# One transposing transfer per attention head in place of two, in an attention, MLP and top-k kernel on one core

## The chip, the cores and the metric

The kernel runs on one core of one Trainium2 chip. The metric is the device time of one execution in microseconds (us); a comparison takes the median of several runs.

## The reference

The input x has four sequences of 512 rows by 512 columns. The first stage adds a 0/1 mask to x: per sequence, the 5120 largest entries of softmax(x) times an outer product, without the diagonal. The second stage is a transformer block with modulated layer norms, sixteen heads of width 128, and an MLP of width 2048 with an exact gelu.

```python
adj = emb_s * emb_t * (softmax(x) / sqrt(n)); adj[diag] = -inf
x = x + one_hot(top_k(adj.flat, 5120))
x1 = ln(x) * (1 + scale1) + shift1
q, k, v = split(x1 @ qkv_w + qkv_b)                 # 16 heads of 128
attn = softmax(einsum('bthd,bshd->bhts', q, k) * DH ** -0.5)
x = x + gate1 * (einsum('bhts,bshd->bthd', attn, v) @ out_w + out_b)
x = x + gate2 * (gelu(ln2(x) @ ffn_w1 + ffn_b1) @ ffn_w2 + ffn_b2)
```

The case's function returns its input plus the block's result once more, and the same weights serve all four sequences.

## The kernel before

Every 32-bit operand is held as a high and a low part, and each product is three matmuls (`mm3`, L1387 to L1389). The four sequences run one after the other (0 to 3); each has a head stage of sixteen heads, an output projection and an MLP. The top-k search of the next sequence is spread over the current one on VectorE and ScalarE. The four 128-row tiles of a head are called row tiles, two of them a pair (`PAIRS` is 2).

TensorE's order is written out by hand. In head h it does the scores of h, the query and key projection of h+1, a v tile or a part of the output projection, and then `attend` of head h-1, which multiplies the transposed probabilities `probT` by v. In head 14 and head 15 there is less to do between the scores and `attend`: head 15 has no projection of a next head, so that `attend` of head 14 follows its scores sooner than in the heads before it. `attend` of head 15 comes later, in the middle of the output projection.

The probabilities of a head reach `probT` in these steps:

- VectorE takes the row maxima (L1217), ScalarE the exponentials (L884), VectorE the reciprocals (L1228).
- ScalarE writes the high float16 half of each row tile into `halves16` (L891). Before the first it waits until the transfers of the head before have landed, since `halves16` is a single buffer for heads 0 to 12 and another for 13 to 15. VectorE writes the low half (L1232) and counts `p16_lo` after each row tile.
- SyncE's queue issues the transposing transfers into `turned16` (L537, function `turn`). Before them it waits for `widened` of the head before and for `p16_lo`.
- GpSimd copies `turned16` into `probT` as 32-bit values, one instruction for each pair (L741, function `widen`), after the pair's transfer has landed and `attend` of the head before is done (`pv_done`). `attend` waits for both.

SyncE's queue works in order. In sequences 1 to 3 the weight loads (`w<-split_weights`, L466) stand between the `turn` of one head and the next. In sequence 0 the weights are split on the chip: after each `turn` come loads of raw weights (`load_raw`, L449) and saves of split ones (L441), each released by a split on GpSimd (L661), which in turn follows a copy on ScalarE (L820). Heads 3, 7, 11 and 15 of sequence 0 have three splits, the others one; the last of the three stands behind `widen` in GpSimd's queue, and ScalarE's copy for it stands ahead of the next head's exponentials.

Of the kernel before, what the change touches and what calls it, by code (L numbers as in the profile page):

```python
# [52 lines left out]
NT = T // P  # L53
# [15 lines left out]
PAIRS = NT // 2  # L69
# [159 lines left out]
def block_kernel(nc, x, cond, weights, ada_w, cols, out):  # L229
    ctx = ExitStack()  # L230
    with ctx:
# [95 lines left out]
        def halves_of(h):  # L327

            return halves16[h >= TURNED_IN_V]

        def turned_of(h):

            return turned16[h >= TURNED_IN_V]
# [12 lines left out]
        def sem(name):  # L346
            return ctx.enter_context(nc.semaphore(name))
# [12 lines left out]
        q_lo, k_lo, v_lo, o_lo = sem("q_lo"), sem("k_lo"), sem("v_lo"), sem("o_lo")  # L360
        scores, nbias_ready, exp_done = sem("scores"), sem("nbias_ready"), sem("exp_done")
        rinv_ready, p16_hi, p16_lo = sem("rinv_ready"), sem("p16_hi"), sem("p16_lo")
        turned_in, widened = [sem("turned_in0"), sem("turned_in1")], sem("widened")
        y_done, y_gated, y_back = sem("y_done"), sem("y_gated"), sem("y_back")
        var_ready, std_ready, z_ready = sem("var_ready"), sem("std_ready"), sem("z_ready")
        zt_done, xt_full, xt_hi, xt_lo = sem("zt_done"), sem("xt_full"), sem("xt_hi"), sem("xt_lo")
# [29 lines left out]
        def wait_apart(eng, signal, value):  # L396


            eng.wait_ge(signal, value)
            eng.sem_inc(waits_met, 1)  # L400
# [32 lines left out]
        def _(sp):  # L433
# [96 lines left out]
            def turn(b, h):  # L530

                k = b * H + h
                for pair in range(PAIRS):
                    if k:
                        wait_apart(sp, widened, (k - 1) * PAIRS + pair + 1)
                    wait_apart(sp, p16_lo, k * NT + 2 * (pair + 1))
                    sp.dma_start_transpose(  # L537
                        turned_of(h)[:, 2 * pair:2 * pair + 2, :, :].rearrange("p i n t -> p (i n) t"),
                        halves_of(h)[:, 2 * pair:2 * pair + 2, :, :].rearrange("p i a s -> p (i a s)"))\
                        .then_inc(turned_in[pair], 16)  # L540

            def first_sequence():
                load_raw(2, AHEAD + 2)
# [11 lines left out]
                for h in range(H):  # L555
                    turn(0, h)
                    if h == H - 1:
                        load_x_again(1)
                    load_raw(at + 2, at + 2 + len(first_splits(h)))
                    at += len(first_splits(h))  # L560
# [17 lines left out]
            def sequence(b, last=False):  # L578
# [7 lines left out]
                for h in range(2, H):  # L586
# [4 lines left out]
                    if h == 14:  # L591
                        load_unit(b, 0)
                    load_qk(b, h)
                turn(b, H - 3)
                load_unit_half(b, 1, 0)
                turn(b, H - 2)
# [35 lines left out]
        def _(pool):  # L632
# [101 lines left out]
            def widen(b, h):  # L734

                k = b * H + h
                for pair in range(PAIRS):
                    wait_apart(pool, turned_in[pair], 16 * (k + 1))
                    pool.wait_ge(pv_done, b * H + h)
                    rows = slice(2 * pair * P, 2 * (pair + 1) * P)  # L740
                    nc.gpsimd.tensor_copy(  # L741
                        probT[:, :, :, rows].rearrange("p a j (i t) -> p i (a j) t", i=2),
                        turned_of(h)[:, 2 * pair:2 * pair + 2, :, :]).then_inc(widened, 1)
# [19 lines left out]
        def _(act_e):  # L763
            def topk_exp(t):

                for i in range(NT):
                    act_e.wait_ge(xmax_ready, t * NT + (i + 1))
                    nc.scalar.activation(adj[:, i, :], adj[:, i, :], ACT.Exp, bias=nxmax[:, i:i + 1],
                                         accum_out=nxsum[:, i:i + 1]).then_inc(xexp_done, 1)

            def topk_count(t, step):

                at = count_split(t)
                src = keys16[:, at:, 1] if step < LEVEL else low[:, at:]
                if t == 1 and step == 0:
                    act_e.wait_ge(rows_saved, 16)
                act_e.wait_ge(cand_ready, t * (STEPS + 1) + (step + 1))
                with nc.allow_low_precision(reason=EXACT):
                    nc.scalar.activation(passed_s[:, :2 * NCOUNT - at], src, ACT.Sign, bias=cand[:, :], scale=-1.0,  # L779
                                         accum_out=cnt_s[:, :]).then_inc(counted_s, 1)  # L780
# [51 lines left out]
            def split_qk(b, h):  # L832

                if h >= 2:
                    split_hi(b, qk_half(h), k_done, b * H + (h - 1))
                else:
                    split_hi(b, qk_half(h), y2_tile, b * OUT_TILES)

            def split_unit(b, u, *halves_of_it):

                for half in halves_of_it or (0, 1):
                    n = unit_half(u, half)
                    if u == 0:
                        split_hi(b, n, v_done, b * H + H)
                    elif u == 1:
                        split_hi(b, n, k_done, b * H + H)
                    elif u in (2, 3) and half == 0:
                        split_hi(b, n, pv_done, b * H + (H - 2 if u == 2 else H))
                    elif u < 6:
                        split_hi(b, n, y_done, b * Y_PIECES + (u - 1 if u < 5 else Y_PIECES))  # L850
                    elif u < 10:
                        split_hi(b, n, f_done, b * KC + 4 * (u - 5))
                    else:
                        split_hi(b, n, y2_half, b * OUT_HALVES + (2 * (u - 10) + half + 1))

            def v_part(b, idx):
                act_e.wait_ge(v_done, b * H + (idx + 1))
                if b and idx == 0:

                    act_e.wait_ge(y2_added, b * OUT_TILES)  # L860
                if idx == QUAD:

                    act_e.wait_ge(out_stored, b * 16 + STORE_CREDIT)
                if idx in (2 * QUAD, 3 * QUAD):

                    act_e.wait_ge(pv_done, b * H + idx - QUAD)
                bk = bank[4 + idx] if idx < 4 else bank[7]
                nc.scalar.mul(v[:, (idx // 4) % 2, 0, idx % 4, :], bk[:, :], V_DOWN).then_inc(v_hi, 1)

            def qk_part(b, h):  # L870
                act_e.wait_ge(q_done, b * H + (h + 1))
                nc.scalar.activation(qk[:, 0, 0, :], bank[4 if h else 1][:, :], ACT.Identity,
                                     bias=col("bq", h))\
                    .then_inc(q_hi, 1)
                act_e.wait_ge(k_done, b * H + (h + 1))
                nc.scalar.activation(qk[:, 1, 0, :], bank[5 if h else 2][:, :], ACT.Identity,  # L876
                                     bias=col("bk", h))\
                    .then_inc(k_hi, 1)

            def head(b, h, last):  # L880
                k = b * H + h
                for i in range(NT):
                    act_e.wait_ge(nbias_ready, b * (H * NT) + (h * NT + i + 1))
                    nc.scalar.activation(prob[:, i, :], bank[i][:, :], ACT.Exp, bias=nbias[:, i:i + 1],  # L884
                                         scale=SCALE, accum_out=rowsum[:, i:i + 1]).then_inc(exp_done, 1)
                if k:
                    for pair in range(PAIRS):
                        act_e.wait_ge(turned_in[pair], 16 * k)
                for i in range(NT):
                    act_e.wait_ge(rinv_ready, k * PAIRS + i // 2 + 1)  # L890
                    nc.scalar.mul(halves_of(h)[:, i, 0, :], prob[:, i, :], rinv[:, i:i + 1]).then_inc(p16_hi, 1)  # L891
                if h + 1 < H:
                    qk_part(b, h + 1)
                if h + 2 < H:
                    split_qk(b, h + 2)
                else:
                    split_unit(b, 1, h - (H - 2))
                if FIRST_TOTAL <= h + 1 and not last:
                    topk_count(b + 1, h + 1 - FIRST_TOTAL)
                if h + QUAD < H:  # L900
                    v_part(b, h + QUAD)
                if h == 0 and not last:
                    topk_exp(b + 1)
                refill(b, h, 0)
                if h:
                    o_part(b, h - 1)
                refill(b, h, 1)

            def o_part(b, h):
                act_e.wait_ge(pv_done, b * H + (h + 1))  # L910
                nc.scalar.activation(act[:, 0, h, :], bank[6][:, :], ACT.Identity, bias=col("bv", h))\  # L911
                    .then_inc(o_hi, 1)

            def refill(b, h, half):

                if h in (3, 7):
                    split_v(b, h // QUAD + 2, half)
                elif h == 11:
                    split_unit(b, 0, half)

            def sequence(b, last=False):
# [8 lines left out]
                for h in range(H):  # L930
                    head(b, h, last)
# [839 lines left out]
```

## Time and profile before

| what | value |
|---|---|
| median of 3 runs | 1572.07 us (1571.55 to 1572.12) |
| profiled execution | 1573.86 us, its span 1572.0 us |
| TensorE (PE) busy | 1508.5 us, 96% |
| VectorE (DVE), ScalarE (ACT), GpSimd (POOL) busy | 1110.1, 886.3, 409.9 us |
| granted TensorE clock, mean | 0.996 |
| queue q1 (all transfers from SyncE) | 325.90 MB, 69.3% of 16 engines' span |

SPq in a row is SyncE's queue issuing a transfer; the second number of a timeline row is how long the instructions took together, and a bracket at its end holds the idle time before it and what ended it. A row ending in x2 is two instructions back to back. Lines (L537) are those of the kernel before.

### The profile page before, as it was taken

What the parts mean: (1) busy time and instruction counts of PE and PEld (TensorE: products, weight loads), DVE (VectorE), ACT (ScalarE), POOL (GpSimd) and SP (SyncE); (2) the same over time, 40 slices, a digit from 0 to 9 for tenths busy, and PEclk for the clock granted to TensorE, in tenths of its full rate; (3) what the DMA queues carried; (4) which work ended last, traced back from release to release, by engine and by line L of the source; (5) the groups of instructions that cost most, each with busy time, mean ns of one, the idle gap of its engine ahead of it and who ended that gap; (6) DMA issues with size and microseconds to landing.
All of it is one profiled execution on the core that took longest, in us unless ns stands there. A gap on an engine that the chain in (4) does not pass through costs nothing.

```text
span 1572.0 us, 21300 instructions
## 1 busy us (share of the span) xinstructions
PE 1508.5 (96%) x7253; PEld 1250.4 (80%) x7253; DVE 1110.1 (71%) x2328; ACT 886.3 (56%) x1631; POOL 409.9 (26%) x243
## 2 busy tenths in 40 slices
PE   1999889999999999999999999999999999999998
PEld 1877778778778888887878888887978888888987
DVE  7878978876786887775775887775777666664431
ACT  4557577774754666663672766664572556554240
POOL 6713635454120322221000232221000122222000
PEclk9999999999999999999999999999999999999999
DMA  7867869998666788685455777677454787776463
GB/s 289 314 242 195 237 171 261 247 219 299 216 231 238 170 214 215 165 206 176 175 219 205 199 207 208 163 214 208 168 201 170 220 201 160 209 210 156 176 237 123
DMA packets 334507, 327.58 MB, mean 208 GB/s; under 512 B 270752, under 2 KB 275008, under 8 KB 331328
## 3 DMA queue, kind: packets, MB, share of 16 engines
q1 hardware_dynamic: 334112, 325.90, 69.3%
q8 instruction: 58, 0.95, 0.2%
q14 instruction: 49, 0.40, 0.1%
q10 hardware_dynamic: 288, 0.33, 0.1%
HBM read 204.54 MB, written 54.54 MB: 165 GB/s over the span
## 4 chain that ended last, share of the span: by engine, by line
PE 87%; DVE 7%; DMA 2%; DVEq 1%; ACT 1%; issue 1%; SPq 1%; POOL 0%; ACTq 0%; POOLq 0%
PE bank L1387 26%; PE bank L1388 26%; PE bank L1389 26%; PE bank L1701 2%; DMA w<-split_weights 1%; DVE halves L1232 1%; DVE tb L1028 1%; PE bank L1604 1%; PE bank L1599 1%; PE bank L1600 1%; PE bank L1416 1%; DVEq L1218 1%; SPq L537 1%; DVE adj L1073 1%; DVE tb L1071 1%
## 5 line engine op out<-in xcount | busy, mean ns | idle before, releaser
L741 POOL CAST probT<-turned 128x2048 fp32r<-128x2048 f16 x128 | 244.3, 1924 | 700.8 <-DMA turned<-halves 395.3
L1387 PE MATMUL bank<-xT,w 128*128 128x512 f32 x704 | 281.0, 399 | 2.0 <-POOL w L661 2.0
L1388 PE MATMUL bank<-xT,w 128*128 128x512 f32 x704 | 275.6, 391 | 0.0
L1389 PE MATMUL bank<-xT,w 128*128 128x512 f32 x704 | 275.3, 391 | 0.0
L884 ACT ACTIVATE prob<-bank,nbias 128x512 f32<-128x512 f32 x256 | 176.4, 690 | 119.8 <-DVE nbias L1219 110.5
L1232 DVE SCALAR_TENSOR_TENSOR halves<-prob,rinv,halves 128x512 f16<-128x512 f32 x256 | 176.7, 752 | 25.2 <-ACT halves L891 24.9
L1217 DVE TENSOR_REDUCE rowmax<-bank 128x1 f32<-128x512 f32 x256 | 174.4, 681 | 0.0
L891 ACT ACTIVATE halves<-prob,rinv 128x512 f16<-128x512 f32 x256 | 164.1, 711 | 17.1 <-DVE rinv L1228 15.3
L1389 PEld LDWEIGHTS bank<-xT,w 128*128 128x128 f32 x704 | 133.0, 189 | 28.2
L1387 PEld LDWEIGHTS bank<-xT,w 128*128 128x128 f32 x704 | 132.9, 189 | 28.0 <-POOL w L661 2.4
L1388 PEld LDWEIGHTS bank<-xT,w 128*128 128x128 f32 x704 | 133.0, 189 | 25.5
L661 POOL TENSOR_TENSOR w<-wraw,w 128x1024 fp32r<-128x1024 f32 x38 | 95.5, 2518 | 179.2 <-ACT w L820 178.9
L1387 PE MATMUL bank<-act,w 128*128 128x512 f32 (+1 forms) x320 | 114.1, 357 | 3.8 <-DMA w<-split_weights 3.8
L1188 DVE SCALAR_TENSOR_TENSOR act<-bank,small,act 128x512 fp32r<-128x512 f32 x64 | 47.9, 748 | 94.6 <-ACT act L911 94.6
L779 ACT ACTIVATE passed_s<-adj,cand 128x1024 bf16<-128x1024 uint16 (+1 forms) x64 | 73.8, 1153 | 70.9 <-DVE cand L1094 41.1
L1388 PE MATMUL bank<-act,w 128*128 128x512 f32 (+1 forms) x320 | 111.5, 348 | 0.0
L1389 PE MATMUL bank<-act,w 128*128 128x512 f32 (+1 forms) x320 | 111.5, 348 | 0.0
L911 ACT ACTIVATE act<-bank,small 128x512 fp32r<-128x512 f32 x64 | 44.0, 688 | 116.0 <-PE bank L1389 115.9
L779 ACT ACTIVATE passed_s<-low,cand 128x1024 bf16<-128x1024 f32 (+1 forms) x64 | 74.0, 1156 | 55.4 <-DVE cand L1094 24.6
L1387 PE MATMUL bank<-qk 128*128 128x512 f32 x256 | 99.9, 390 | 5.5 <-DVE qk L1188 5.2
L1387 PE MATMUL bank<-w,act 128*128 128x512 f32 x256 | 101.5, 396 | 0.0
L1188 DVE SCALAR_TENSOR_TENSOR qk<-bank,small,qk 128x512 fp32r<-128x512 f32 x128 | 90.3, 744 | 14.9 <-ACT qk L876 8.6
(173 smaller groups left out, 3342.4 us busy)
## 6 DMA issues: line engine op xcount, KB each, us to landing
w<-split_weights SPq DMA_DIRECT2D x154, 1024.0 KB, 6.0
split_weights<-w SPq DMA_DIRECT2D x38, 1024.0 KB, 6.7
wraw<-weights_in SPq DMA_DIRECT2D x48, 512.0 KB, 4.8
split_weights<-xT SPq DMA_DIRECT2D x7, 1024.0 KB, 7.8
adaw<-ada_w_in SPq DMA_DIRECT2D x4, 1536.0 KB, 12.6
xr<-x_in SPq DMA_DIRECT2D x4, 1024.0 KB, 6.3
split_weights<-qk SPq DMA_DIRECT2D x3, 1024.0 KB, 7.8
adj<-x_in SPq DMA_DIRECT2D x3, 1024.0 KB, 7.9
```

The lines of the kernel that those rows point to most:

```text
L661: nc.gpsimd.tensor_tensor(w[:, region, 1, span], wraw[:, k % 2, :], w[:, region, 0, span].bitcast(F32), ALU.subtract)\
L741: nc.gpsimd.tensor_copy(probT[:, :, :, rows].rearrange("p a j (i t) -> p i (a j) t", i=2), turned_of(h)[:, 2 * pair:2 * pair + 2, :, :]).t ...
L779: nc.scalar.activation(passed_s[:, :2 * NCOUNT - at], src, ACT.Sign, bias=cand[:, :], scale=-1.0, accum_out=cnt_s[:, :]).then_inc(counted_ ...
L884: nc.scalar.activation(prob[:, i, :], bank[i][:, :], ACT.Exp, bias=nbias[:, i:i + 1], scale=SCALE, accum_out=rowsum[:, i:i + 1]).then_inc( ...
L891: nc.scalar.mul(halves_of(h)[:, i, 0, :], prob[:, i, :], rinv[:, i:i + 1]).then_inc(p16_hi, 1)
L911: nc.scalar.activation(act[:, 0, h, :], bank[6][:, :], ACT.Identity, bias=col("bv", h))\
L1188: return V.scalar_tensor_tensor(dst, src, bias, hi.bitcast(F32), ALU.add, ALU.subtract)
L1217: V.reduce_max(rowmax[:, i:i + 1], bank[i][:, :], AX.X)
L1232: V.scalar_tensor_tensor(halves_of(h)[:, i, 1, :], prob[:, i, :], rinv[:, i:i + 1], halves_of(h)[:, i, 0, :], ALU.mult, ALU.subtract).then ...
L1387: pe.matmul(dst, w_hi_ap, x_hi_ap, start=first, stop=False)
L1388: pe.matmul(dst, w_hi_ap, x_lo_ap, start=False, stop=False)
L1389: return pe.matmul(dst, w_lo_ap, x_hi_ap, start=False, stop=last)
```

## The change

`turn` issues one transposing transfer over all four row tiles where it issued two over pairs. It waits for `widened` of both pairs of the head before and for `p16_lo` of all four row tiles. `turned_in` is one semaphore, and both copies of `widen` and ScalarE's wait use its full count. `widen` still has two instructions.

```diff
-        turned_in, widened = [sem("turned_in0"), sem("turned_in1")], sem("widened")
+        turned_in, widened = sem("turned_in"), sem("widened")
@@ def turn(b, h):
-                for pair in range(PAIRS):
-                    if k:
-                        wait_apart(sp, widened, (k - 1) * PAIRS + pair + 1)
-                    wait_apart(sp, p16_lo, k * NT + 2 * (pair + 1))
-                    sp.dma_start_transpose(
-                        turned_of(h)[:, 2 * pair:2 * pair + 2, :, :].rearrange("p i n t -> p (i n) t"),
-                        halves_of(h)[:, 2 * pair:2 * pair + 2, :, :].rearrange("p i a s -> p (i a s)"))\
-                        .then_inc(turned_in[pair], 16)
+                if k:
+                    wait_apart(sp, widened, k * PAIRS)
+                wait_apart(sp, p16_lo, (k + 1) * NT)
+                sp.dma_start_transpose(turned_of(h)[:, :, :, :].rearrange("p i n t -> p (i n) t"),
+                                       halves_of(h)[:, :, :, :].rearrange("p i a s -> p (i a s)"))\
+                    .then_inc(turned_in, 16)
@@ def widen(b, h): for pair in range(PAIRS):
-                    wait_apart(pool, turned_in[pair], 16 * (k + 1))
+                    wait_apart(pool, turned_in, 16 * (k + 1))
@@ ScalarE, def head(b, h, last): if k:
-                    for pair in range(PAIRS):
-                        act_e.wait_ge(turned_in[pair], 16 * k)
+                    act_e.wait_ge(turned_in, 16 * k)
```

## Rows read from the trace of the kernel before

**Rows 1.** The page: the costliest group; busy us, mean ns, idle before it, and what ended it.

```profile
L741 POOL CAST probT<-turned 128x2048 fp32r<-128x2048 f16 x128 | 244.3, 1924 | 700.8 <-DMA turned<-halves 395.3
```

**Rows 2.** Waits on PE, 500 to 900 us, the longest: us in total, times, longest.

```profile
PE bank L1387 <- DMA w<-split_weights: 2.3, 1, 2.3
```

**Rows 3.** All instructions on the tile turned (durations in ns).

```profile
L537 SPq DMA_TRANSPOSE turned<-halves x128: 1323/2282/5597, 126.8 to 1438.1; - x128
...
DMA to landing us min/median/max: 4.2/4.7/9.1
```

**Rows 4.** Windows from the first issue in Rows 6: us, clock, DMA share, GB/s.

```profile
697.93:699.20 1.27, 1.00 0.04 8
699.20:704.50 5.30, 1.00 1.10 202
```

**Rows 5.** Timeline of sequence 1, head 8, and the next head's scores, halves and issues.

```profile
608.45 0.39 PE L1387 MATMUL bank<-qk 128*128 128x512 f32 x1
616.69 5.38 SPq L537 DMA_TRANSPOSE turned<-halves  x2
622.22 0.39 PE L1387 MATMUL bank<-qk 128*128 128x512 f32 x1
625.37 1.90 POOL L741 CAST probT<-turned 128x2048 fp32r<-128x2048 f16 x1 [1.02 <-DMA turned<-halves]
628.75 2.56 ACT L891 ACTIVATE halves<-prob,rinv 128x512 f16<-128x512 f32 x4 [0.16 <-DVE rinv L1228]
631.02 4.45 SPq L537 DMA_TRANSPOSE turned<-halves  x2
633.27 0.39 PE L1387 MATMUL bank<-probT,v 128*128 128x512 f32 x1
```

**Rows 6.** Timeline of sequence 1, head 14, from its scores to its attend.

```profile
689.69 0.39 PE L1387 MATMUL bank<-qk 128*128 128x512 f32 x1
696.41 2.74 DVE L1232 SCALAR_TENSOR_TENSOR halves<-prob,rinv,halves 128x512 f16<-128x512 f32 x4 [0.47 <-ACT halves L891]
697.93 4.98 SPq L537 DMA_TRANSPOSE turned<-halves  x2
706.63 1.91 POOL L741 CAST probT<-turned 128x2048 fp32r<-128x2048 f16 x1 [1.72 <-DMA turned<-halves]
709.07 0.39 PE L1387 MATMUL bank<-probT,v 128*128 128x512 f32 x1
```

**Rows 7.** Timeline of head 14 in sequences 0, 2 and 3: last copies, and attend.

```profile
342.02 1.90 POOL L741 CAST probT<-turned 128x2048 fp32r<-128x2048 f16 x1 [1.94 <-DMA turned<-halves]
344.06 0.47 PE L1387 MATMUL bank<-probT,v 128*128 128x512 f32 x1
...
1070.38 1.90 POOL L741 CAST probT<-turned 128x2048 fp32r<-128x2048 f16 x1 [0.33 <-DMA turned<-halves]
1074.21 0.39 PE L1387 MATMUL bank<-probT,v 128*128 128x512 f32 x1
...
1428.41 3.75 POOL L741 CAST probT<-turned 128x2048 fp32r<-128x2048 f16 x2 [9.17 <-PE bank L1389]
1434.30 0.39 PE L1387 MATMUL bank<-probT,v 128*128 128x512 f32 x1
```

**Rows 8.** Timeline of sequence 0, heads 8 and 12.

```profile
260.34 3.74 POOL L741 CAST probT<-turned 128x2048 fp32r<-128x2048 f16 x2 [4.22 <-DMA turned<-halves]
265.47 0.39 PE L1387 MATMUL bank<-probT,v 128*128 128x512 f32 x1
...
300.95 1.05 ACT L820 CAST w<-wraw 128x1024 fp32r<-128x1024 f32 x1 [3.83 <-DMA wraw<-weights_in]
...
318.29 2.57 ACT L891 ACTIVATE halves<-prob,rinv 128x512 f16<-128x512 f32 x4 [1.75 <-DMA turned<-halves]
320.68 0.47 PE L1387 MATMUL bank<-probT,v 128*128 128x512 f32 x1
324.48 0.47 PE L1387 MATMUL bank<-qk 128*128 128x512 f32 x1 [0.83 <-DVE qk L1188]
```

## The prediction

> **What bounds the kernel now.** I read the page first: TensorE is busy for 1508.5 of the span's 1572.0 us, 96%, so what matters is whether a step makes TensorE wait. The copies into `probT` on GpSimd are the costliest single group after the matmuls, but GpSimd is idle for 700.8 us ahead of them [rows 1], so their busy time costs nothing by itself.
>
> Then the waits on TensorE, stretch by stretch. In the head stage of sequence 0 TensorE waits for VectorE's low parts of q and k, as for 0.83 us at 324.48 [rows 8]. In sequence 1 its longest wait is 2.3 us for a weight load [rows 2]. Nowhere does it wait for a copy into `probT`: the way from `halves16` over the transfer to `attend` is hidden in all 64 heads. The question is by how much, so I went through the timeline head by head and took, for each `attend`, its start minus the end of the second copy.
>
> In an ordinary head this slack is large: the copy that starts at 625.37 ends at 627.27, and `attend` starts at 633.27, 6.0 us later [rows 5]. Head 14 differs. In sequence 1 the second copy ends at 708.54 and `attend` starts at 709.07, a slack of 0.53 us [rows 6]; in sequences 0, 2 and 3 it is 0.14, 1.93 and 2.14 us [rows 7]. Two heads of sequence 0 are near too: head 8 with 1.39 us, and head 12, whose `attend` starts at 320.68, with 0.15 us [rows 8]. All other heads have 1.4 us or more, most of them 4 to 7.
>
> **The change, part by part.**
>
> *The wait for the row tiles.* VectorE's four low halves of a head take 2.74 us, from 696.41 to 699.15 [rows 6]. Before, the first transfer went out after two of them; now the only one goes out after four, that is 2.74/2 = 1.37 us later. The wait for `widened` of the head before is met: in an ordinary head the copies would end at 630.5 (worked out below), and the next issue, at 631.02 + 1.37 = 632.4 [rows 5], is later by 1.9 us.
>
> *The transfer itself.* Two issues back to back took 4.98 us for head 14 and 5.38 us for head 8 [rows 5, 6]; one issue has a median of 2.28 us and lands a median of 4.7 us after it [rows 3]. What moves is 1 MiB (128 partitions x 4 row tiles x 2 halves x 512 x 2 bytes). The windows from the first issue show almost no traffic for 1.27 us and then 5.3 us of full queues at 202 GB/s [rows 4]; 1.05 MB at 202 GB/s is 5.2 us. So the data begins about 1.3 us after the issue starts, before the first instruction ends, and its length is that of the data, not of the number of instructions. I take it that one instruction moves 1 MiB as two did: from first issue to last landing 697.93 to about 706.6, 8.7 us [rows 6], and in other heads about 7.0, which is 2.3 us of issue plus the median landing of 4.7 [rows 3]. Bounds: not under 6.6 us unless the data itself goes faster (the shortest landing, 4.2, plus 2.4 to 2.6 for the second half's data), not over 9.1 + 2.6 = 11.7.
>
> *The first copy loses its start.* Before, GpSimd widened the first pair while the second was in flight; now both copies, 1.9 us each, stand behind the one landing. So where the second copy was waiting for its transfer, as in sequence 1 [rows 6], its end moves by 1.37 + 1.9 = 3.2 to 3.3 us. I take 3.2. GpSimd sets nothing else here but the splits of sequence 0.
>
> *SyncE's queue.* The weight loads behind `turn` go out 1.4 us later. In sequences 1 to 3 they are for heads two or more on, at 13.77 us a head (scores at 608.45 and 622.22 [rows 5]), so that is hidden. ScalarE's wait for the transfer of the head before: it starts the next head's halves at 628.75 [rows 5]; the transfer would be issued at 616.69 + 1.37 = 618.1 and land by 618.1 + 8.7 = 626.8. Hidden, by 2 us. If it were not, the softmax of every head would be late.
>
> *Ordinary heads.* The copies would end at 626.8 + 3.75 = 630.5 against an `attend` at 633.3 [rows 5]: hidden by 2.8 us. The first head of each of sequences 1 to 3 has an `attend` some 3 us sooner than that (slack 3.1 to 3.5 us by the same subtraction), so it comes out at zero, with 0.2 us each as the upper bound.
>
> *Head 14 of each sequence.* Stall = 3.2 less the slack: sequence 0, 3.2 - 0.14 = 3.1; sequence 1, 3.2 - 0.53 = 2.7; sequence 2, 3.2 - 1.93 = 1.3; sequence 3, 3.2 - 2.14 = 1.1. Sum 8.2 us. Behind `attend` on TensorE's queue stands the output projection, so all of it moves the end; its later waits (the 2.3 us [rows 2]) are for loads that themselves follow an `attend`, and move along. `attend` of head 15 is then late by the same stall, and its own copies end before it: no second stall.
>
> *Sequence 0, heads 7 to 12.* Here the transfers go through queues full of raw loads and saves: the load behind `turn` of head 11 is what ScalarE waits 3.83 us for at 300.95, and right behind that copy stand the exponentials of head 12 [rows 8]. The load goes out 1.4 us later, so the softmax of head 12, its transfer and ScalarE's wait at 318.29 (already 1.75 us for a transfer) move by 1.4. Head 12: landing 318.2 + 1.4, copies until 319.6 + 3.75 = 323.4, against 320.68: 2.7 us, of which the 0.83 us that TensorE waits anyway at 324.48 is absorbed: 1.9 us. Head 8 in the same way: both copies ran without a gap from 260.34, so its second landing was at 262.2 at the latest and, by the end of its issue, at 261.6 at the earliest; with 1.4 more and 3.75 of copies that is 266.8 to 267.4 against 265.47: 1.6 us. After head 3 a similar late load is covered by a wait of 4 us of ScalarE for VectorE. Together 3.5 us; from both sides 1 (the full queues hide the late issue) to 6 us (the late copies delay GpSimd's split and with it the next load).
>
> **Sum.** 8.2 + 3.5 = 11.7 us. The profiled execution has 1573.86 us, 1.9 us of it outside its span, so such an execution would take 1585.6. The median of the runs is 1572.07, 1.8 below the profiled one: 1583.8 us, +0.74%.
>
> **A rule that speaks against this.** The row shows 202 GB/s for the transposed data [rows 4]. The Trainium skill's page "Advanced Engine Details and Errata", section "X-Bar Transpose (TRN2)", expects 350 to 400 GB/s, and its page "DMA: Bandwidth & Descriptors", section "Rules for kernel authors", says to coalesce many small transfers into one large one, best 1 MiB or more. By that rate, as an estimate, 1.05 MB take 2.8 us in place of 5.2, and nearly all stalls above would go. By that rule the trace does not go: the engines' share over the stretch of both transfers is 1.10 [rows 4], so they were full, with no gap that coalescing could close. What it would do here is the first rival.
>
> **The rivals.**
>
> *A faster single transfer, no slowdown.* If one instruction has its data moved quicker, the landing follows sooner. The point from which it decides is in the timeline of head 14 [rows 6]: issue at 699.3, copies must start by 709.07 - 3.75 = 705.3, so 6.0 us from issue to landing (5.6 in sequence 0). With the data in 3 us in place of 5.2, 7.0 becomes 4.8 and 8.7 becomes 6.5: stalls of 0 to 0.9 us, 1572 to 1575 us. Against it: the data rate looks like a limit of the queues, not of the issues. 13 in 100; a further 3 for a real gain in sequence 0, whose full queues would then drain sooner (1565 to 1569).
>
> *The softmax loop becomes the bound.* If one large instruction has to be written out whole before its data moves, issue to landing becomes 4.5 + 5.2 + 2 = 11.7 us. ScalarE may not write the next halves before the landing. From its first half to the issue are 2.3 us (628.75 to 631.02 [rows 5]) plus 1.37, 3.6; the loop closes at 3.6 + 11.7 = 15.3 us against 13.77 a head. From a landing of 10.1 us on each head grows; at 11.7 by 1.5 us, 60 times, 90 us: 1660 us. Against it: the data started before the first instruction had ended [rows 4]. 6 in 100.
>
> *Slow landings in all four sequences.* With 8.7 us in sequences 2 and 3 as well, their stalls are about 2.8 each, and with the upper bound of sequence 0: 1589. This is the upper part of my case.
>
> **How the numbers follow.** Slower by stalls at head 14 and in sequence 0: 78 in 100, 1576 to 1590; no slowdown 16, of these 3 faster; the loop 6. Its likeliest point is 1583.8. The range from 1573.8 to 1590 takes in part of the rival. About 0.2% (3 us) is what this kernel's measurement tells from no change: faster 0.04, same 0.12, slower 0.84.
>
> **What the profile after would show.** 64 issues of about 4.6 us at L537, 1.4 us later in each head; a landing of 7 to 9 us; waits of TensorE, new in this profile, ended by GpSimd's copy (L741) in head 14 of each sequence, 1 to 3 us each, and in heads 8 and 12 of sequence 0; ordinary heads still 13.77 us. Landings under 6 us, or heads longer than 13.8 us, would show me wrong.

## The result and the profile after

The changed kernel takes 1646.24 us (1642.77 to 1649.76, 4 runs) against 1572.09 (1571.55 to 1572.53, 4 runs): ratio 1.0472, 95% interval 1.0449 to 1.0494. It is slower by 74 us, where I had forecast 11.7. The profiled execution took 1642.77 us, its span 1641.0. Two executions that stand far off all others of their kernel, one of 3037 us of the kernel before and one of 5123 us of a run below, are left out of the ratios.

First, all instructions on the tile `turned`; a duration is shortest, median, longest in ns.

```profile
L536 SPq DMA_TRANSPOSE turned<-halves x64: 4715/4844/7720, 128.2 to 1504.2; - x64
...
DMA to landing us min/median/max: 6.7/6.7/9.8
```

Against [rows 3]: half as many issues, each about as long as two (2 x 2.28 us), and a landing 6.7 us after the issue. Windows from one issue on (us, clock, DMA share, GB/s) have the shape of [rows 4]:

```profile
617.16:618.40 1.24, 1.00 0.02 3
618.40:623.60 5.20, 1.00 1.12 210
```

So the transfer did what I took it to do. The 74 us are elsewhere. The costliest groups of the page (busy us, mean ns, idle before):

```profile
L739 POOL CAST probT<-turned 128x2048 fp32r<-128x2048 f16 x128 | 247.9, 1965 | 790.2 <-DMA turned<-halves 790.2
...
L1229 DVE SCALAR_TENSOR_TENSOR halves<-prob,rinv,halves 128x512 f16<-128x512 f32 x256 | 232.7, 970 | 22.4 <-ACT halves L888 18.8
...
L1223 DVE TENSOR_SCALAR rowsum<-rowsum 128x2 f32<-128x2 f32 x128 | 106.4, 831 | 19.3 <-ACT prob L882 16.4
```

VectorE's low halves had a mean of 752 ns before and have 970 now; `rowsum`, a scaling of two numbers in each partition, had 295 ns and has 831. No operand of theirs was changed. The groups of VectorE in the kernel before:

```profile
L1232 DVE SCALAR_TENSOR_TENSOR halves<-prob,rinv,halves 128x512 f16<-128x512 f32 x256 | 176.7, 752 | 25.2 <-ACT halves L891 24.9
...
L1226 DVE TENSOR_SCALAR rowsum<-rowsum 128x2 f32<-128x2 f32 x128 | 37.8, 295 | 19.1 <-ACT prob L884 16.2
```

The timeline of two ordinary heads of the changed kernel shows where they stand:

```profile
603.34 4.82 SPq L536 DMA_TRANSPOSE turned<-halves  x1
...
610.22 3.75 POOL L739 CAST probT<-turned 128x2048 fp32r<-128x2048 f16 x2 [10.07 <-DMA turned<-halves]
...
610.81 0.15 DVE L1216 TENSOR_SCALAR nbias<-rowmax 128x1 f32<-128x1 f32 x1
...
611.41 0.73 DVE L1223 TENSOR_SCALAR rowsum<-rowsum 128x2 f32<-128x2 f32 x1
...
612.30 1.69 DVE L1223 TENSOR_SCALAR rowsum<-rowsum 128x2 f32<-128x2 f32 x1
614.07 0.17 DVE L1225 RECIPROCAL rinv<-rowsum 128x2 f32<-128x2 f32 x1
614.32 2.74 DVE L1229 SCALAR_TENSOR_TENSOR halves<-prob,rinv,halves 128x512 f16<-128x512 f32 x4
...
617.16 4.73 SPq L536 DMA_TRANSPOSE turned<-halves  x1
...
625.71 4.21 POOL L739 CAST probT<-turned 128x2048 fp32r<-128x2048 f16 x2 [11.75 <-DMA turned<-halves]
...
626.44 5.34 DVE L1229 SCALAR_TENSOR_TENSOR halves<-prob,rinv,halves 128x512 f16<-128x512 f32 x4 [0.46 <-ACT halves L888]
...
631.88 4.84 SPq L536 DMA_TRANSPOSE turned<-halves  x1
```

The copies run from 610.22 to 613.97. The second rowsum starts at 612.30 and ends at 613.99, with the copies; alone it takes 0.17 us. In the next head the copies come a little later and meet the low halves: these take 5.34 us in place of 2.74. A scaling of one column (nbias, 610.81) beside the same copy takes its 0.15 us. In [rows 5] the copies ended at 627.27, and VectorE's rowsum of that head started at 628.23: it missed them by one microsecond.

Two more things differ. The first is the waits on PE (us in total, times, longest). The largest of all, 27.5 us for `tb` in the top-k search ahead of sequence 0, was there before (27.4); these three have grown. Before, `probT` had none, the weight loads 3.8 us and `qk` 5.2. The second is the granted clock about one of them:

```profile
PE bank L1384 <- POOL probT L739: 21.7, 9, 5.0
PE bank L1384 <- DMA w<-split_weights: 18.0, 18, 2.3
PE bank L1384 <- DVE qk L1185: 11.8, 6, 3.2
```

```profile
720.00:744.00 24.00, 18.80 (x85) 0.99 0.78 208
744.00:752.00 8.00, 7.78 (x22) 0.60 0.68 128
```

At 744.22 TensorE had waited 4.95 us to begin `attend` of head 14, and the granted clock of the 8 us from 744 on is 0.60. In shorter windows it is 0.50, the lower level of 1.2 GHz, from 744 to 750. That is six us at half speed, by my estimate 3 us lost. Before, no wait of TensorE stood there. The mean granted clock is 0.986, before 0.996.

Where does TensorE lose the time? I took the start of each `attend` in both traces. In sequence 1, from `attend` of head 0 to that of head 15, TensorE needs 217.6 us where it needed 199.4. The steps to most heads are what they were, 13.8 us (603.25, 617.02, 630.78). The added 18.2 us are 4.7 at head 3, 1.9 at head 7, 1.3 at head 11, 5.8 at head 14 and 3.0 at head 15, this one with the low clock in it, and 1.5 for all others. The chain of work that ended last shows how heads 3 and 7 come in. A row is start, duration and what ran; here it is from the low halves at 626.44 to the weight load that is waited for ahead of `attend` of head 7:

```profile
626.44 4.02 DVE halves L1229 x2
...
631.88 4.84 SPq L536
...
637.47 7.46 DMA w<-split_weights
...
644.98 0.51 PE bank L1384
```

The held low halves make the issue late, the weight load stands behind that issue in SyncE's queue, and TensorE waits for the load.

### The profile page after: what moved, and what is told of

The parts are those of the page before. It is cut to its first block, busy times and chain, and to the rows that moved or that the text cites. A ratio compares the mean times of both kernels' runs of the same rounds, so it can differ in the third digit from the quotient of the medians.

```text
span 1641.0 us, 21109 instructions
## 1 busy us (share of the span) xinstructions
PE 1532.9 (93%) x7253; PEld 1256.8 (77%) x7253; DVE 1226.9 (75%) x2328; ACT 889.5 (54%) x1631; POOL 413.9 (25%) x243
## 4 chain that ended last, share of the span: by engine, by line
PE 50%; DVE 21%; DMA 11%; DVEq 9%; issue 3%; SPq 2%; ACT 2%; POOL 1%; ACTq 0%; POOLq 0%
PE bank L1384 14%; PE bank L1385 14%; PE bank L1386 14%; DVE halves L1229 9%; DMA turned<-halves 7%; DVEq L1215 4%; DMA w<-split_weights 3%; DVEq L1224 3%; PE bank L1698 2%; SPq L536 2%; DVE tb L1025 2%; DVEq L1233 1%; DVE rowsum L1223 1%; DVE nbias L1216 1%; DVE qk L1185 1%
## 5 line engine op out<-in xcount | busy, mean ns | idle before, releaser
L739 POOL CAST probT<-turned 128x2048 fp32r<-128x2048 f16 x128 | 247.9, 1965 | 790.2 <-DMA turned<-halves 790.2
L1229 DVE SCALAR_TENSOR_TENSOR halves<-prob,rinv,halves 128x512 f16<-128x512 f32 x256 | 232.7, 970 | 22.4 <-ACT halves L888 18.8
L888 ACT ACTIVATE halves<-prob,rinv 128x512 f16<-128x512 f32 x256 | 167.9, 713 | 54.5 <-DVE rinv L1225 44.3
L1384 PE MATMUL bank<-probT,v 128*128 128x512 f32 x256 | 104.1, 406 | 21.8 <-POOL probT L739 21.7
L1223 DVE TENSOR_SCALAR rowsum<-rowsum 128x2 f32<-128x2 f32 x128 | 106.4, 831 | 19.3 <-ACT prob L882 16.4
L777 ACT ACTIVATE passed_s<-low,cand 128x1024 bf16<-128x1024 f32 (+1 forms) x64 | 74.0, 1156 | 55.0 <-DVE cand L1091 24.7
L1385 PE MATMUL bank<-probT,v 128*128 128x512 f32 x256 | 102.7, 401 | 0.0
```

Of the source, the lines that this page charges most:

```text
L739: nc.gpsimd.tensor_copy(probT[:, :, :, rows].rearrange("p a j (i t) -> p i (a j) t", i=2), turned_of(h)[:, 2 * pair:2 * pair + 2, :, :]).t ...
L1223: V.tensor_scalar(rowsum[:, two], rowsum[:, two], 1.0 / P_UP, None, ALU.mult)
L1229: V.scalar_tensor_tensor(halves_of(h)[:, i, 1, :], prob[:, i, :], rinv[:, i:i + 1], halves_of(h)[:, i, 0, :], ALU.mult, ALU.subtract).then ...
L1384: pe.matmul(dst, w_hi_ap, x_hi_ap, start=first, stop=False)
L1385: pe.matmul(dst, w_hi_ap, x_lo_ap, start=False, stop=False)
```

## The experiments

I set three theories against each other. Theory A: the copies, moved later, lie over VectorE's operations on SBUF and hold them. Theory B: the single large transfer itself costs. Theory C: the lateness of `probT` and of the weight loads costs. The kernel before ran beside each group of runs, at 1572 to 1574 us.

**Both parts of the timing, one by one.** Two transfers as before, but issued after all four row tiles; then two transfers issued as before, but both copies after both landings; then both.

```diff
 # late issue, in turn
-                    wait_apart(sp, p16_lo, k * NT + 2 * (pair + 1))
+                    wait_apart(sp, p16_lo, (k + 1) * NT)
 # late copy, in widen
-                    wait_apart(pool, turned_in[pair], 16 * (k + 1))
+                    for other in range(PAIRS):
+                        pool.wait_ge(turned_in[other], 16 * (k + 1))
```

> The kernel before, with one part of the change alone: both transfers of a pair each are issued only after all four row tiles are written. Theory A (what costs is when GpSimd's copies run: moved later, they lie over VectorE's operations on SBUF, rowsum and the low halves, and block them): the second copy of a head ends 19 to 20 us after its scores, just reaching the next head's rowsum at 19.5, so a small part of the 74 us: 1576 to 1590 us. Theory B (the single large transfer itself costs, by its longer issue or its landing, not its timing): no part of the 74 us is here, 1572 to 1577 us.

> The kernel before, with the other part alone: two transfers issued as before, but GpSimd's first copy of a head waits for both landings, as it must with one transfer. Theory A: landing of the second transfer at 15.3 to 17 us after the scores, copies until 19 to 20.7, again just reaching VectorE's rowsum of the next head: 1576 to 1595 us. Theory B: 1572 to 1577 us.

> The kernel before, with both parts: two transfers, but issued after all four row tiles, and both copies after both landings. All timing of the changed kernel without its single transfer. Theory A: copies at 17 to 22 us after the scores as in the changed kernel, low halves at some 970 ns mean, 1635 to 1650 us. Theory B: only the stalls at head 14 that I had predicted, 1580 to 1590 us, low halves at 750 ns.

Measured: late issue 1581.41 us (ratio 1.0059, 1.0040 to 1.0079); late copy 1593.94 (1.0138, 1.0116 to 1.0160); both 1638.0 (1.0416, 1.0386 to 1.0446). Low halves 756, 794 and 960 ns, rowsum 431, 799 and 902 ns. All as theory A had it. With two transfers and the late timing 66 of the 74 us are there, so it is not the single transfer; theory B is left with about 8 us. The parts don't add (9 + 22 against 66). By the means, each alone moves the copies at most onto the rowsums (431 and 799 ns) and hardly onto the low halves (756 and 794); both together move them onto these too (960).

**The copies an eighth as wide.** The changed kernel, with this in `widen`; seven eighths of the transposed probabilities are left out in all heads but the first of a sequence:

```diff
-                        probT[:, :, :, rows].rearrange("p a j (i t) -> p i (a j) t", i=2),
-                        turned_of(h)[:, 2 * pair:2 * pair + 2, :, :]).then_inc(widened, 1)
+                        probT[:, :, :, rows].rearrange("p a j (i t) -> p i (a j) t", i=2)[:, :, :, 0:P // 8 if h else P],
+                        turned_of(h)[:, 2 * pair:2 * pair + 2, :, 0:P // 8 if h else P]).then_inc(widened, 1)
```

> The changed kernel, with GpSimd's copies into probT an eighth as wide in all heads but the first of each sequence (the rest of the transposed probabilities is left out, so the output is not the reference's). Transfers, issues and waits are those of the changed kernel. Theory A: rowsum back to 0.3 us and low halves to 0.75 us mean, no stall at head 14; what is left are the waits for v loads: 1576 to 1592 us. Theory B: the transfers are as large and as late as in the changed kernel, so VectorE's operations stay slow and the time stays over 1620 us.

Measured: 1571.95 us, ratio 0.9996 (0.9983 to 1.0009), a little less than the 1576 to 1592 of theory A. The waits for weight loads fell too, from 18.0 to 6.1 us, and none for `probT` is left. Groups of VectorE and waits on PE:

```profile
L1229 DVE SCALAR_TENSOR_TENSOR halves<-prob,rinv,halves 128x512 f16<-128x512 f32 x256 | 177.9, 756 | 25.1 <-ACT halves L888 24.4 <-issue 0.4
...
L1223 DVE TENSOR_SCALAR rowsum<-rowsum 128x2 f32<-128x2 f32 x128 | 32.0, 250 | 22.8 <-ACT prob L882 19.8
```

```profile
PE bank L1384 <- DMA w<-split_weights: 6.1, 5, 2.0
```

With short copies the single transfer, its late issue and its landing cost nothing. But this run also has `probT` ready 3 us sooner, so it does not tell A from C.

**The block alone.** The kernel before, with the copies of heads 0 to 12 of sequences 1 to 3 held back onto the next head's low halves, and nothing else edited.

```diff
                     pool.wait_ge(pv_done, b * H + h)
+                    if pair == 0 and 0 < b and h < H - 3:
+                        wait_apart(pool, rinv_ready, (k + 1) * PAIRS + 1)
```

> The kernel before, two transfers issued as before; only GpSimd's first copy of heads 0 to 12 in sequences 1 to 3 waits in addition for VectorE's first reciprocal of the next head, so that the copies lie over the low halves. Transfers, their issues and the weight loads are not touched, and head 14 is not held. Theory A (overlap of GpSimd's copies and VectorE's operations on SBUF blocks VectorE): low halves over 1000 ns mean in these sequences, slower by 25 us or more, 1597 to 1660 us. Theory C (what costs is the late arrival of the probabilities at attend and the late loads): copies at 20 to 24 us against an attend at 24.8, no stall, 1572 to 1578 us.

Measured: 1607.34 us, ratio 1.0207 (1.0173 to 1.0240), low halves 1037 ns. Timeline:

```profile
607.81 4.21 POOL L743 CAST probT<-turned 128x2048 fp32r<-128x2048 f16 x2 [10.19 <-DVE rinv L1230]
622.21 4.20 POOL L743 CAST probT<-turned 128x2048 fp32r<-128x2048 f16 x2 [10.18 <-DVE rinv L1230]
```

```profile
608.53 5.36 DVE L1234 SCALAR_TENSOR_TENSOR halves<-prob,rinv,halves 128x512 f16<-128x512 f32 x4 [0.48 <-ACT halves L893]
622.92 5.35 DVE L1234 SCALAR_TENSOR_TENSOR halves<-prob,rinv,halves 128x512 f16<-128x512 f32 x4 [0.48 <-ACT halves L893]
```

The same 5.3 us as in the changed kernel, and 14.39 us from head to head where it was 13.77. Waits for `probT` are 5.2 us in all, so theory C's 1572 to 1578 is out. The block costs time with early transfers too, though by another way than in the changed kernel: the chain of work from 608.53 on stays on VectorE but for 0.73 us, from the held low halves over the low parts of q and k, a step of the search and the row maxima to the next low halves. So here VectorE sets the time of a head, not the late transfer. This run shows that the block costs time, but not how much of the 74 us it is.

**Copies cut into four.** The changed kernel, each copy as four of 128x512.

```diff
-                    nc.gpsimd.tensor_copy(
-                        probT[:, :, :, rows].rearrange("p a j (i t) -> p i (a j) t", i=2),
-                        turned_of(h)[:, 2 * pair:2 * pair + 2, :, :]).then_inc(widened, 1)
+                    for i in (2 * pair, 2 * pair + 1):
+                        for a in range(2):
+                            copy = nc.gpsimd.tensor_copy(probT[:, a, :, i * P:(i + 1) * P],
+                                                         turned_of(h)[:, i, a * NT:(a + 1) * NT, :])
+                    copy.then_inc(widened, 1)
```

> The changed kernel with each of GpSimd's copies (1.9 us) cut into four of a quarter (about 0.5 us), the same bytes at the same time. Theory A, with the block lasting to the end of the copy under way: VectorE is held for at most one short copy at a time, low halves near 0.85 us mean, 1600 to 1630 us. If only the total overlap counted, not the length of one copy: 1640 to 1655 us.

Measured: 1644.73 us (1.0452, 1.0425 to 1.0478), low halves 974 ns, rowsum 354 ns. This missed my 1600 to 1630. Rowsum was let in. The longest low half fell from 2893 to 1156 ns, so each is held for no more than one short copy, but more of them are held: the median rose from 748 to 1093 ns. And a short copy takes 620 ns, so that the eight of a head take at least 5.0 us against 3.75, beside VectorE 5.5 to 6.4 (as from 622.75 to 629.12), and TensorE waits 45.3 us for them.

**Fills in place of copies.** Seven eighths of each copy become a fill of `probT`: GpSimd writes as much and reads little.

```diff
+                    part = P // 8 if h else P
+                    if h:
+                        nc.gpsimd.memset(probT[:, :, :, rows].bitcast(F32)
+                                         .rearrange("p a j (i t) -> p i (a j) t", i=2)[:, :, :, part:P], 0.0)
...
-                        probT[:, :, :, rows].rearrange("p a j (i t) -> p i (a j) t", i=2),
-                        turned_of(h)[:, 2 * pair:2 * pair + 2, :, :]).then_inc(widened, 1)
+                        probT[:, :, :, rows].rearrange("p a j (i t) -> p i (a j) t", i=2)[:, :, :, 0:part],
+                        turned_of(h)[:, 2 * pair:2 * pair + 2, :, 0:part]).then_inc(widened, 1)
```

> The changed kernel; in all heads but the first of a sequence each of GpSimd's copies is replaced by a fill of seven eighths of its part of probT and a copy of the last eighth (so most of the transposed probabilities is left out, and the output is not the reference's). GpSimd is busy about as long as in the changed kernel, and probT is ready as late, but it reads an eighth. Theory A with the block only where GpSimd reads SBUF: low halves near 0.78 us mean, and only the stalls of late readiness at head 14, 1578 to 1600 us. Theory A with the block on any work of GpSimd on SBUF: as the changed kernel, 1635 to 1650. Theory C: 1635 to 1650 too.

Measured: 1612.03 us, ratio 1.0248 (1.0221 to 1.0275), between the two forecasts. Low halves are free, 761 ns; rowsum is not, 825 ns. GpSimd and VectorE of one head:

```profile
613.47 1.59 POOL L741 MEMSET probT<- 128x1792 f32 x1 [9.49 <-DMA turned<-halves]
615.01 0.40 POOL L743 CAST probT<-turned 128x256 fp32r<-128x256 f16 x1
615.35 1.60 POOL L741 MEMSET probT<- 128x1792 f32 x1
```

```profile
613.67 1.42 DVE L1227 TENSOR_SCALAR rowsum<-rowsum 128x2 f32<-128x2 f32 x1
615.16 0.17 DVE L1229 RECIPROCAL rinv<-rowsum 128x2 f32<-128x2 f32 x1
615.24 1.72 DVE L1227 TENSOR_SCALAR rowsum<-rowsum 128x2 f32<-128x2 f32 x1
```

The rowsums end at 615.09 and 616.96, with the fills (615.06, 616.95). So there are two blocks here: the low halves, with two inputs in SBUF, wait for the copies, which read SBUF, and not for the fills; the two-column rowsum waits for the fills, which only write, as well.

**v loads from another queue.** The changed kernel; the v loads for heads 8 and 12 of sequences 1 to 3 go out from ScalarE's queue.

```diff
 # SyncE's sequence
-                    if h % QUAD == 2 and h < 14:
+                    if h == 2:
 # ScalarE's head, behind v_part(b, h + QUAD)
+                if b and h in (3, 7):
+                    for j in range(2):
+                        n = v_half(h // QUAD + 2, j)
+                        act_e.dma_start(w_place(n), scratch[n]).then_inc(w_in[PLACE[n]], 16)
```

> The changed kernel with the v loads for heads 8 and 12 of sequences 1 to 3 issued from ScalarE's queue right after the v tile that frees their place, not behind the transposing transfer on SyncE's queue. Theory A (the waits for these loads follow from the late transfers, which follow from the blocked VectorE): the waits of TensorE for them, about 12 us, go, but the softmax is as late as before, so 1632 to 1645 us. If the loads themselves were the cause of the slowdown: under 1610 us.

Measured: 1657.15 us (1.0545, 1.0506 to 1.0583), slower still and outside my 1632 to 1645. The waits for loads fell to 5.8 us, but the loads now go out ahead of the transfer (571.57 against 574.17 for head 3, whose issue took 7.57 us), the median landing rose from 6.7 to 7.1 us, and the waits for `probT` rose to 36.3 us. The loads were not the cause; they are one place where the late issue reaches TensorE.

**Rowsum and head 14.** Three runs on the changed kernel (TensorE's work moved ahead of `attend` of head 14; rowsum by columns; both) and two on the kernel before.

```diff
 # TensorE, head 15
                     wide(b, "out", 0, 9, KC - 2, y_done)
+                    wide(b, "out", 1, 0, 6, y_done)
@@ sequence, behind the heads
-                wide(b, "out", 1, 0, 6, y_done)
 # rowsum by columns
-                    V.tensor_scalar(rowsum[:, two], rowsum[:, two], 1.0 / P_UP, None, ALU.mult)
+                    for i in (2 * pair, 2 * pair + 1):
+                        V.tensor_scalar(rowsum[:, i:i + 1], rowsum[:, i:i + 1], 1.0 / P_UP, None, ALU.mult)
```

> The changed kernel; TensorE does the first six column blocks of the next part of the output projection (4.1 us) ahead of attend of head 14, not behind it. The stall there was 4.9 us in sequences 0 to 2 and 3.0 in sequence 3, and TensorE's clock fell to its lower level during it. Theory A: the stall of head 14 goes, that of head 15 grows by up to 2.5 us, the clock stays up: 1620 to 1640 us, the 40 us or so of the ordinary heads stay. If the stall at head 14 and its clock were most of the 74 us: under 1600.

> The changed kernel; VectorE scales the row sums in two operations on one column each, not in one on two columns. In the changed kernel's trace the two-column form waits for GpSimd's copy, and one-column operations beside a copy do not. Theory A: rowsum free (0.15 us each), but the low halves still wait for the copies, so the loop from issue over landing and copies to the next issue gets shorter only by what of rowsum and reciprocal stood behind the copies: 1625 to 1646 us. If the loop were closed by rowsum alone: under 1610.

> The changed kernel with one-column row sums and with TensorE's work moved ahead of attend of head 14. The two alone gave 1632.6 and 1638.3 against 1646.2. Theory A: both gains nearly add, since one shortens the loop in all heads and the other covers the stall of one: 1620 to 1630 us, still far over the kernel before, because the low halves are still held by the copies.

Measured: 1638.31 us (1.0408, 1.0389 to 1.0426) with a mean granted clock of 0.993; 1632.56 (1.0370, 1.0354 to 1.0386); both 1623.91 (1.0325, 1.0286 to 1.0364). In the second run the 256 one-column rowsums have a mean of 148 ns, and the low halves rise to 1121 ns: they now come sooner and wait longer. All three lie where theory A put them; 7.9 and 13.7 us alone are 22.3 together, so the two gains add. With the first edit the clock stays at 1.00 from 744 to 752 and no wait for `probT` is longer than 2.8 us; that gives back 7.9 of the 74 us.

> The kernel before with both edits of the two runs ahead of this: row sums in one-column operations, and TensorE's work moved ahead of attend of head 14. Before, TensorE waited in sequence 0 for q and k parts some 5 us, behind operations of VectorE that stood behind GpSimd's copies and splits. Theory A: some of that goes, 1567 to 1573 us.

> The kernel before with row sums in one-column operations alone. Theory A: VectorE busy falls by some 15 us of blocked rowsum, TensorE's waits in sequence 0 shrink by 0 to 4 us: 1568 to 1573 us.

Measured: both edits 1572.25 us, ratio 0.9992 (0.9978 to 1.0006), no difference; rowsum by columns alone 1570.83, ratio 0.9983 (0.9973 to 0.9992). The kernel before had its own small share of the block: rowsum took 37.8 us in all, and 27.2 in one-column form. The second interval lies just below the kernel before, by 0.17%, but the first run has the same edit and shows no gain, so that a gain in time is likely and not shown.

**Lateness with nothing blocked.** Fills and one-column rowsums together, on the changed kernel (the two diffs above).

> The run with fills in place of seven eighths of each copy (most of the transposed probabilities is left out, and the output is not the reference's), and the row sums in one-column operations as well. GpSimd is as busy and probT is ready as late as in the changed kernel, but nothing of VectorE should be held. Theory A: what is left is the lateness alone, that is the stalls I had predicted: 1578 to 1590 us. If lateness by itself, not the block of rowsum, makes up the 40 us between the short copies (1572) and the fills (1612): 1605 to 1615.

Measured: 1593.77 us (1.0139, 1.0101 to 1.0177); rowsum 148 ns, low halves 799 ns. VectorE's and TensorE's rows:

```profile
L1234 DVE SCALAR_TENSOR_TENSOR halves<-prob,rinv,halves 128x512 f16<-128x512 f32 x256 | 189.2, 799 | 22.7 <-ACT halves L892 22.7
L1228 DVE TENSOR_SCALAR rowsum<-rowsum 128x1 f32<-128x1 f32 x256 | 27.1, 148 | 25.2 <-ACT prob L886 21.8 <-issue 0.6
```

```profile
PE bank L1389 <- POOL probT L743: 14.2, 6, 3.0
PE bank L1389 <- DMA w<-split_weights: 6.1, 6, 2.7
```

A little over my forecast, and well under the 1605 of the other reading. The 14.2 us of waits for `probT` are 2.2 us at each of heads 8 and 12 of sequence 0, and 2.8, 2.8, 3.0 and 1.3 us at head 14 of the four sequences. Theory C has its part of the 74 us too, then, some 22. The ladder: short copies 1572.0; copies as late as in the changed kernel that hold almost nothing (low halves 799 ns), 1593.8, +22; with rowsum held by fills, 1612.0, +18; with the low halves held by copies that read, 1646.2, +34.

## Why the prediction was wrong

**The transfer: right.** 64 issues of 4.84 us, landing after 6.7 us at best and in the median, 1 MiB in 5.2 us at 210 GB/s. The rule of 350 to 400 GB/s (the Trainium skill, "Advanced Engine Details and Errata", "X-Bar Transpose (TRN2)") is not borne out by this case, and one large transfer was no faster than two.

**"GpSimd sets nothing else here but the splits of sequence 0": the step that failed.** I moved the copies by 3.2 us and asked only who waits for their result. I did not ask what VectorE does at their new place: the sum has no term for it, and by the ladder the two blocks are 18 + 34 = 52 of the 74 us. The Trainium skill's page "SBUF — State Buffer", section "Who interferes with whom", has the rule: VectorE and GpSimd share one pair of SBUF ports, locked for a whole instruction; an operation of VectorE with two SBUF inputs contends with a GpSimd instruction that reads SBUF, and one in a two-port mode with any. The traces agree in both halves: low halves 970 ns beside copies, 761 beside fills; two-column rowsum 831 and 825 ns, one-column 148. No view names the mode of an instruction, so that the two-column rowsum is in a two-port mode is not shown. The sign of the block was in the trace of before, where rowsum had a mean of 295 ns at a median of 169 and a longest of 1895.

**"Ordinary heads: hidden by 2.8 us": right for TensorE there, wrong for what follows.** The copies that end at 613.97 have their `attend` at 617.02, 3.0 us later, and most heads still take 13.8 us. But the block closes a loop that I did not have: issue, landing, copies, the low halves of the next head behind them, next issue. By the timeline above: 617.16, landing 8.55 us later at 625.71, copies until 629.92, low halves until 631.78, issue at 631.88. That is 14.7 us a turn against 13.77 for TensorE; with a landing of 6.9 us (603.34 to 610.22) the turn is 13.8. The next copies end at 629.92, only 0.9 us ahead of their `attend`. So a slow landing leaves all that follows later against TensorE, and TensorE pays where the slack is small: at the weight loads at heads 3, 7 and 11, and at head 14.

**The rival of the loop** (90 us, at 6 in 100) had the right shape and the wrong link: it closed over ScalarE's wait and needed a landing of 10.1 us. ScalarE waited 9.2 us in all for landings; the link was the block, and 6.7 to 8.6 us of landing were enough. That its 90 us are near the 74 is luck: it had every head slower by 1.5 us.

**Head 14 and sequence 0: right in kind, and in size without the block.** For head 14 I had 3.1, 2.7, 1.3 and 1.1 us; measured were 4.88, 4.95, 4.89 and 3.02. Its own VectorE operations were held: in sequences 0 to 2 its two rowsums (724.66 and 726.54 in sequence 1, 1.7 us each in place of 0.17), in sequence 3 its low halves (5.45 us). With nothing blocked the stalls are 2.8, 2.8, 3.0 and 1.3, and with heads 8 and 12 of sequence 0 (4.4 where I had 3.5) they sum to 14.2 us against my 11.7. Only the term of sequence 2 was far off. The rest of the 22 us of that run I had put at nothing. Part of it is the clock: after the stall of 2.8 us in sequence 1 it was at 0.50 from 724 to 726.

**"Loads are for heads two or more on": wrong for v.** The v loads issued behind `turn` of heads 3 and 7 are for the very next head. TensorE waited 18.0 us for weight loads in 18 places, 11 of them for v and 7 for the output projection. But with short copies 6.1 us are left: the waits follow from the late `turn`.

**What stays open:** the 8 us between two transfers with the late timing (1638.0) and one (1646.2), and why some landings take 8.6 us and others 6.9. Neither was tried by itself. The intervals of the first two lie close (ratios to 1.0446 and from 1.0449), so the 8 us may be less. How the 74 us split between the blocks, the lateness and the clock is told by the ladder in that order only; in another order the steps could have other sizes, as the two parts of the timing did.

## What to carry to other kernels

When an edit moves work of GpSimd in time, look at what VectorE runs at the new place, not only at who waits for the result: here an operation with two SBUF inputs, and a scaling of two columns, were held until GpSimd's instruction ended. A tiny instruction whose mean was well over its median was the mark of it in the profile. Then ask where the lateness comes out: here not in the ordinary heads, but where slack was small, at loads that stand behind the late issue and at head 14. Merging two transfers gave no bandwidth here, and took away the overlap of the first with what produces and what uses it.

## What the runs showed of the hardware

- A scaling of 128x2 numbers in SBUF took 1.69 us beside a copy and 1.72 us beside a pure fill; split into two of 128x1 it took 0.148 us each, with either beside it.
- GpSimd is held too: two copies back to back over the low halves took 4.21 us against 3.75.
- Four copies of 128x512 at 620 ns take 2.48 us where one of 128x2048 takes 1.90. Beside the short ones no low half took more than 1156 ns.
- A stall of TensorE of 4.95 us was followed by a granted clock of 0.60 over 8 us; in the run with nothing blocked a stall of 2.8 us was followed by 0.50 over 2 us.
